# Attention with a mixture of experts on one core: two of eight half-chunks of the shared expert are computed at the end of the program instead of in its setup

## What is computed

```python
xn = _layernorm(x)
# attention
s = einsum('bthd,bshd->bhts', q, k) * scale
logits = 2 * log(abs(s) + 1e-30) + log_G[:, :, :, None] - log_G[:, :, None, :]
a = exp(where(mask, logits, -inf) - m)              # m: row maximum
y = num / (sum(a) + 1e-6)                           # num = a @ v
y = (y - mean(y)) / sqrt(var(y) + 1e-9) * ln_w      # per head
attn = y.reshape(B, T, hq * d) @ w_proj
# mixture of experts, h = layernorm(xn) * g + b
ye = einsum('ecf,efd->ecd', silu(xe @ W1) * (xe @ W3), W2)
routed = zeros.at[tok].add(ye[idx, pos] * gate)
shared = silu(h @ W1s) * (h @ W3s) @ W2s            # the part that moves
out = x + attn + routed + shared
```

## Time and profile before

| | before |
|---|---|
| median of the runs (lowest to highest) | 1029.54 us (1028.38 to 1030.29) |
| span of the profiled execution | 1027.0 us |
| TensorE busy | 959.8 us, 93% |
| VectorE busy | 876.1 us, 85% |
| ScalarE busy | 676.7 us, 66% |
| GpSimd busy | 631.0 us, 61% |
| chain that ended last | TensorE 72%, VectorE 16%, GpSimd 4% |

### The profile page before, as it was taken

The page is one execution under the profiler, slowest core; times in us unless marked ns, Lnnn a source line. Parts: engine busy times, 40 slices in busy tenths (PEclk is TensorE's granted clock), DMA queues, the critical chain, the costliest instruction groups (busy, mean ns, idle before and its releaser), DMA issues.

```text
span 1027.0 us, 23345 instructions
## 1 busy us (share of the span) xinstructions
PE 959.8 (93%) x8871; PEld 707.3 (69%) x8871; DVE 876.1 (85%) x1730; ACT 676.7 (66%) x1077; POOL 631.0 (61%) x593
## 2 busy tenths in 40 slices
PE   3999989899999999999999999999999999999964
PEld 2675567567676767687777677777768677768643
DVE  5668738899999998998999898988898989898892
ACT  1243447676766677868778867787876877886731
POOL 0320438889898966666658566748575856766711
PEclk9999999999999999999999999999999999999996
DMA  9401105443434354454444344435434535433540
GB/s 262 102 1 47 51 12 146 106 107 95 108 98 101 101 135 111 104 135 119 104 126 124 97 126 107 119 82 143 104 98 118 127 85 133 112 97 96 147 125 22
DMA packets 77952, 108.66 MB, mean 106 GB/s; under 512 B 15853, under 2 KB 46445, under 8 KB 77712
## 3 DMA queue, kind: packets, MB, share of 16 engines
q1 hardware_dynamic: 72768, 104.50, 39.3%
q0 software_dynamic: 5072, 2.67, 1.9%
HBM read 31.61 MB, written 11.36 MB: 42 GB/s over the span
## 4 chain that ended last, share of the span: by engine, by line
PE 72%; DVE 16%; POOL 4%; issue 4%; ACT 2%; DMA 1%; SPq 1%; POOLq 0%; DVEq 0%; ACTq 0%
PE PS L545 19%; PE PS L737 19%; PE PS L770 18%; PE PS L540 6%; DVE PS L1336 3%; PE PS L588 3%; PE PS L591 3%; PE PS L598 3%; DVE U L1336 2%; DVE PS L1329 2%; POOL U L1439 1%; DVE SM L1361 1%; DVE U L1300 1%; POOL xe_d L1471 1%; PE PS L561 1%
## 5 line engine op out<-in xcount | busy, mean ns | idle before, releaser
L737 PE MATMUL PS<-Qt,Kt 64*128 64x256 f32 (+1 forms) x2560 | 276.8, 366 | 13.5 <-POOL Qt L1442 9.4
L737 PEld LDWEIGHTS PS<-Qt,Kt 64*128 64x128 f32 x2560 | 229.7, 188 | 52.9 <-POOL Qt L1442 11.3
L916 ACT ACTIVATE U<-PS 128x1024 f32<-128x1024 f32 x144 | 140.9, 1023 | 62.5 <-PE PS L737 58.7
L1439 POOL TENSOR_TENSOR U<-U,consts 128x512 f32<-128x512 f32 x96 | 126.2, 1315 | 45.5 <-DMA U<-U 45.5
L770 PE MATMUL PS<-U 128*64 128x256 f32 (+1 forms) x1344 | 139.8, 349 | 0.2 <-ACT U L912 0.2
L1461 POOL TENSOR_SCALAR_AFFINE_SELECT U<-U 128x256 f32<-128x256 f32 x128 | 61.8, 560 | 102.9 <-ACT U L841 102.6
L770 PEld LDWEIGHTS PS<-U 128*64 128x64 f32 x1344 | 93.2, 137 | 40.2 <-issue 5.7
L1507 POOL TENSOR_TENSOR U<-U,SM 128x1024 f32<-128x1024 f32 x32 | 72.2, 2257 | 68.0 <-DVE SM L1356 68.0
L1336 DVE SCALAR_TENSOR_TENSOR PS<-U,ES,PS 128x512 f32<-128x512 f32 x144 | 108.4, 752 | 4.7
L1300 DVE SCALAR_TENSOR_TENSOR U<-PS,U 128x768 f32<-128x768 f32 x96 | 88.3, 952 | 26.2 <-PE PS L737 23.9
L841 ACT ACTIVATE U<-U,negG 128x256 f32<-128x256 f32 (+1 forms) x256 | 98.7, 455 | 5.6 <-DMA U<-H_d 5.3
(11 more groups left out here) (177 smaller groups left out, 1890.7 us busy)
## 6 DMA issues: line engine op xcount, KB each, us to landing
G<-U SPq DMA_DIRECT2D x512, 64.0 KB
U<-U SPq DMA_DIRECT2D x192, 128.0 KB
U<-H_d SPq DMA_DIRECT2D x32, 512.0 KB
Kt<-Kt SPq DMA_DIRECT2D x32, 256.0 KB, 3.9
U<-in_w SPq DMA_DIRECT2D x21, 256.0 KB
acc<-in_x SPq DMA_DIRECT2D x4, 512.0 KB, 5.5
ye_d<-G SPq DMA_DIRECT2D x4, 512.0 KB, 8.0
U<-ye_d SPq DMA_DIRECT2D x4, 512.0 KB, 5.3
```

Of the source, the lines that this page charges most:

```text
L737: mm = te.matmul(bank[:, 256 * n:256 * n + 256 - lo], Kt[u % 2][(ki + hd) % 2][rows, 128 * j:128 * j + 128], Qt[p % 2][m // 2][rows, 256 * ...
L916: s.activation(A[n % NA], PS[:, first:first + 1024], ACT.Square, scale=0.125, bias=GUARD).then_inc(a_so, 1)
L1439: g.tensor_tensor(sw, sw, sinT[:, cols], ALU.mult).then_inc(made, 1)
```

## The change

Half-chunks 6 and 7 leave the setup (NSH is 6, so that all counts of silus, products and additions that others wait for shrink). Their h lies in a part of its own of the buffer U (HX), which other buffers are moved by 256 columns for. In pair 31's ticks three jobs are new. "sload" on SyncE loads the three weight matrices again, into the place of the raw and swapped queries, when the last rotation is done. "sup" is one of 16 products of 512 columns on TensorE; each even one is followed by a silu on ScalarE, each odd one by a product on VectorE. "sdn" is the down product, here in one piece of 16 products of 128 columns for a half-chunk, and its addition on VectorE. Half-chunk 6 is sup 0 to 7 and sdn 0, half-chunk 7 is sup 8 to 15 and sdn 1.

The times of other jobs are changed in all pairs: on TensorE y 1 and wp, on ScalarE y 0, fin and ysq, on VectorE fold, wp, sum and root, on GpSimd combine, n1 and n2.

```diff
+NTAIL = 2
+NSH = 8 - NTAIL
-            ("rt", 41.4, 27.8, 1.12, 4, 2), ("up", 33.04, 24.16, 6.2, 8, 4), ("down", 66.9, 24.8, 6.12, 8, 2),
+            ("rt", 41.4, 27.8, 1.12, 4, 2), ("up", 33.04, 24.16, 6.2, NSH, 4), ("down", 66.9, 24.8, 6.12, NSH, 2),
...
-POOL_AT = [(51.94, "combine", 0), (66.52, "combine", 1), (67.43, "combine", 2), (-5.62, "select", 0),
...
-           (3.66, "vs", 3), (30.16, "n1", 0), (38.34, "n2", 0), (-21.4, "k", 0), (-15.9, "k", 1), (-15.66, "q", 0),
+POOL_AT = [(52.31, 'combine', 0), (67.78, 'combine', 1), (71.29, 'combine', 2), (-5.62, 'select', 0), (-4.73, 'select', 1), (-2.85, 'select', 2), (1.22, 'select', 3), (-16.1, 'vs', 1), (-6.13, 'vs', 2), (3.66, 'vs', 3), (30.22, 'n1', 0), (42.54, 'n2', 0), (-21.4, 'k', 0), (-15.9, 'k', 1), (-15.66, 'q', 0), (-9.41, 'q', 1)]
...
+    if kind in ("sload", "sup", "sdn"):
+        return p == 31
...
+        HX = [U[:, 6144 + 512 * i:6656 + 512 * i] for i in range(NTAIL)]
+        TW = [U[:, 512 * i:512 * i + 512] for i in range(3)]
+        TG = [[RAWk[:, 0:512], RAWk[:, 512:1024], SWPk[:, 0:512], SWPk[:, 512:1024]],
+              [Kt[0][i][:, 512 * j:512 * j + 512] for i in range(2) for j in range(2)]]
...
+                elif kind == "sload":
+                    sp.wait_ge(s_sq, 64 * 32)
+                    sp.wait_ge(g_q, 64)
+                    sy.dma_start(TW[0], w1s).then_inc(s_tw, 16)
+                    sy.dma_start(TW[1], w3s).then_inc(s_tw, 16)
+                    sy.dma_start(TW[2].rearrange("p (c n) -> p c n", c=4),
+                                 w2s.rearrange("(c p) n -> p c n", p=128)).then_inc(s_tw, 16)
...
+                elif kind == "sup":
+                    c, n = divmod(job[2], 8)
+                    f, w = divmod(n, 2)
+                    pb = bank_of(job)
+                    pe.wait_ge(s_tw, 48)
+                    te.matmul(pb[:, :], TW[w][:, 128 * f:128 * f + 128], HX[c], start=True, stop=True).then_inc(p_su, 1)
+                elif kind == "sdn":
+                    c = job[2]
+                    pb = bank_of(job)
+                    for q in range(4):
+                        for f in range(4):
+                            pe.wait_ge(v_su, 4 * c + f + 1)
+                            mm = te.matmul(pb[:, 128 * q:128 * q + 128], TG[c][f][:, 128 * q:128 * q + 128],
+                                           TW[2][:, 128 * f:128 * f + 128], start=f == 0, stop=f == 3)
+                    mm.then_inc(p_sn, 1)
...
                 if un < 3:
-                    ac.wait_ge(p_sd, 8)
-                    ac.wait_ge(p_cb, 32)
+                    ac.wait_ge(p_sd, NSH)
+                    ac.wait_ge(p_cb, 4 * NSH)
                     ac.wait_ge(p_rt, 4)
...
+                elif kind == "sup":
+                    c, f = divmod(job[2], 4)
+                    ac.wait_ge(p_su, 8 * c + 2 * f + 1)
...
+                    s.activation(TG[c][f], P[BANK["sup", 31, 8 * c + 2 * f]][:, :], ACT.Silu).then_inc(a_su, 1)
...
+                elif kind == "sup":
+                    c, f = divmod(job[2], 4)
+                    ve.wait_ge(p_su, 8 * c + 2 * f + 2)
+                    ve.wait_ge(a_su, 4 * c + f + 1)
+                    v.tensor_tensor(TG[c][f], TG[c][f], P[BANK["sup", 31, 8 * c + 2 * f + 1]][:, :], ALU.mult).then_inc(v_su, 1)
```

92 lines of the change are left out of this document (50 added, 42 removed), and 3 rows, old and new, of the table PE_AT.

## The result

The changed kernel takes 1065.6 us (median of 4 runs, 1058.3 to 1070.0) against 1029.8 (the median of 4 runs too): a ratio of 1.034, 95% interval 1.029 to 1.038. It is slower by 3.4%; the forecast was 1018.4, in a range of 1012.5 to 1025.0. The profiled execution has a span of 1059.8 us, 32.8 over that of before.

The account below looks back on a forecast made before the run. TensorE was taken to bound setup and loop, a VectorE, GpSimd and ScalarE chain the tail. Terms -11.8 + 1.0 - 0.8 + 0.5 = -11.1 us gave span 1015.9, plus 2.54 for the median: 1018.4 us, range 1012.5 to 1025.0.

Parts of the forecast that it names:

- the loop term: Loop: moving the second norm multiplication behind the last selection on GpSimd loses 1.0 us, in pairs 1, 3, 5 and 7.
- The bound of 7.6 us: Loop: upper bound on the loss from the moved norm multiplication, 4 x 1.9 us.
- two meetings in the tail: Tail: GpSimd's norm multiplications held up beside VectorE; two such meetings could cost 1.8 us, 0.4 was charged.
- GpSimd sets the pace: Rival, loop pairs 1 to 8: 7.6 us lost instead of 1.0, so 1025.0 us; chance 0.11.
- VectorE carries the moved work on the chain: Rival, tail: all ten moved VectorE instructions in line, tail +6.9 us, time 1024.8 us; chance 0.09.
- above 1037: Upper end of the slowest rival: clock stays at 1.2 GHz through the tail, 1031.3 to 1037 us; chance 0.05.
- Setup: Before the loop: two half-chunks removed, 13.3 us saved less 1.5 for the clock, so 11.8 us.
- the second stall: First scores: TensorE's 2.0 us standstill after 24 score matmuls, waiting behind the decay rows, goes away.
- The wait before pair 31: Before pair 31's first scores: TensorE's 1.99 us wait for the rotation shrinks, 0.8 us saved, between 0 and 2.
- The tail: End of kernel: last transposes 1.2 us later, 1.1 gained back, 0.4 for clock dips: 0.5 us lost, between -1.5 and +4.
- a down product: Tail: each moved down product on TensorE was costed at 1.8 us.
- the sign that the prediction named for a wrong tail term: Tail: the term is wrong if the last transposes wait for product 14 and not for GpSimd.

Follow-up runs that it names:

- e4: The kernel before with only the second norm multiplication moved behind the fourth selection (42.54 instead of 38.34): 1067.7 us, ratio 1.036.
- e3: The changed kernel with only the second norm multiplication put back at 38.34, ahead of the fourth selection: 1025.4 us, ratio 0.996.
- g1: The kernel before with the second norm multiplication moved to 42.54 and a bare GpSimd wait for VectorE's root in its old place: 1039.9 us, ratio 1.010.
- g2: The kernel before with the second norm multiplication moved and cut to 128 of 1024 columns, plus a bare wait for VectorE's root at 38.34: 1025.0 us.
- h3: The changed kernel with the second norm multiplication back at 38.34 and the shared expert's tail work left out: 1022.4 us, ratio 0.994.
- h4: As t1, with VectorE's first tail product ahead of the fold and the tail's down product computed twice: 1017.6 us, ratio 0.988.
- t1: The changed kernel with the second norm multiplication back at 38.34 and one half-chunk in the tail instead of two: 1021.9 us, ratio 0.991.
- t2: The changed kernel with the second norm multiplication back at 38.34 and VectorE's first tail product ahead of pair 31's fold: 1024.7 us, ratio 0.996.

## Why the prediction was wrong

**The step that failed** is the loop term, in the paragraph on the moved norms: "GpSimd comes to the selection 1.9 us early, can't use them, and does the multiplication after it", hence 1.0 us. I costed the move by GpSimd's capacity and slack in pairs 1, 3, 5 and 7 alone. Measured, it is 38 to 40 us (e4; after less e3), through the root in the odd pairs and through the first steps in all. Three things were missing.

- *Whom it passes.* n2 moved from 38.34 to 42.54. Between those numbers lies not only the selection at 41.22 but, in the odd pairs, the key rotation at 38.6 (-21.4 of the pair three later). I named the selection and not the rotation, though the order of instructions shows it. And n2 carried a wait for VectorE's root; what stood behind it was held by that wait, and the price of letting it go is what g1 and g2 give back, 28 and 38 us.
- *What runs beside it.* The bound of 7.6 us was four times n2's duration. It has no term for what GpSimd does to VectorE. Yet I had weighed exactly this in the tail: n2 at 2.81 us and the fold at 2.27 instead of 0.7. The Trainium skill, SBUF — State Buffer, section "SBUF: two separate sides", says that the two engines shut each other out only where VectorE's instruction has two SBUF inputs or a two-port mode. The trace agrees: 0.17 us steps take up to 1.28 beside a 1.27 us rotation, and everything with an input in PSUM keeps 719 to 721 ns on average in all kernels of the table. I weighed two meetings in the tail, and not those of the same instruction in every pair of the loop.
- *Who is full.* At 95 of 100 us early in the loop and 90 later, VectorE had 70 us of idle time in the whole loop, the gaps between its instructions counted in. Of 56 us more of busy time only 16 came out of it.

The rival "GpSimd sets the pace" (1025.0) was about this move, but with the wrong engine as the bound, and so too small. "VectorE carries the moved work on the chain" had the right engine and the wrong work. No case of mine reached above 1037.

**Setup** was right in its sum, 11.8 us forecast and 11.3 there, and in its mechanism: the rotation on GpSimd as the next limit, the second stall gone, the clock at 0.50 costing 1.5 us. That the sum fits so well is in part luck: the scatters did not keep their place but came 1.7 us earlier, so that the projection of pair 1 was 13.7 us earlier and not 11.8, and the wait for VectorE within pair 0, which the forecast did not have, took 2.3 back.

**The wait before pair 31** (-0.8) is read from e3, which is the changed kernel without the move of n2: it fell from 1.99 to 1.57 us, so 0.4 was gained, and the scores behind it took 4.12 us instead of 5.65. But from their start to the maximum of pair 31 e3 needs 1.8 us more than before, where 0.6 to 1.0 was expected.

**The rest of the loop.** In e3 the loop to pair 29 lost 3.2 us against before. The kernels with the same order in the loop lost 0.5 (h3, h4), 1.2 (t1) and 3.1 (t2), so its size is not steady, and its cause stays open. One place of it is a meeting as above, at the maximum of pair 7. In e3 VectorE's first step started 0.04 us ahead of the first norm multiplication and took 2.49 us:

```profile
357.64 2.49 DVE L1372 SCALAR_TENSOR_TENSOR PS<-AX,ES 128x512 f32<-128x512 f32 x1
```

```profile
357.68 1.90 POOL L1552 TENSOR_TENSOR U<-U,SM 128x1024 f32<-128x1024 f32 x1 [4.00 <-DVE SM L1399]
```

Before, it had 0.16 us of lead, kept its 0.70, and GpSimd paid:

```profile
369.65 0.70 DVE L1329 SCALAR_TENSOR_TENSOR PS<-AX,ES 128x512 f32<-128x512 f32 x1
```

```profile
369.81 2.29 POOL L1507 TENSOR_TENSOR U<-U,SM 128x1024 f32<-128x1024 f32 x1 [3.88 <-DVE SM L1356]
```

**The tail** went as told in its order, and the clock stayed at 1.00 as forecast: transposes 1.04 us for 1.0, each output projection 1.97 for 1.85. In e3 the last transposes came 0.7 us later against the maximum of pair 31; 1.2 had been charged in all, the maximum's own delay included, which alone was 1.3 us from the maximum of pair 29. One term was mis-sized: a down product stands with 1.8 us in my sum, and takes 3.7 to 3.8, the 3.85 of the earlier trace rows; there are two. A matmul of this code has two records in the trace (the x2 of one product in the earlier trace rows). The 16 products of a down product in the tail are the same 32 records that half-chunk 5 has in the earlier trace rows, and not half of them; likewise the change takes 32 products of 128 columns out of setup, which are 64 records. TensorE ran from 996.5 to its last projection without a gap. The second down product counted in full. The first put product 14 to 1007.39 and the last transposes behind it to 1008.25, where GpSimd had ended at 1007.42: that is the sign that the prediction named for a wrong tail term. These are rows of e3, TensorE's and then GpSimd's last n2:

```profile
996.45 0.66 PE L548 MATMUL PS<-consts,U 128*128 128x128 f32 x4 [3.19 <-DVE U L1300]
...
1003.82 3.73 PE L720 MATMUL PS<-U 128*128 128x128 f32 x32
...
1012.07 3.84 PE L720 MATMUL PS<-U,Kt 128*128 128x128 f32 x32
```

```profile
1005.52 1.90 POOL L1556 TENSOR_TENSOR U<-U,SM 128x1024 f32<-128x1024 f32 x1 [4.69 <-DVE SM L1422]
```

The tail with the pairs ahead of it cost e3 1.3 + 1.7 = 3.0 us, instead of 0.5. Not all of that is the moved work: h3, which has none of it in the tail, still lost 1.3 there. With 0.9 us less in setup, 3.0 more in the loop (3.2 instead of the 0.2 of its two terms) and 2.5 more in the tail, the 1018.4 becomes 1024.8; e3 is at 1025.4. Of the 47 us between forecast and result, then, 40 are one table entry, and 7 are the other terms.

## What to carry to other kernels

Before moving an instruction in a queue, list everything that it passes, and for each of those what it had been waiting behind: a wait that looks like a cost can be the gate that keeps two engines apart. Where VectorE is near full, price GpSimd's two-input work by what stands beside it (two inputs in SBUF, or one in PSUM), in every repetition of the loop and not only at its ends. And a chain at the end of the program that leaves TensorE idle pays twice, by the wait and by the clock behind it; filling the hole, even with work that is thrown away, made the projection behind it 2.9 us shorter here.
